# Loading the weights between later chunks of x, one shifted group sum, and score vectors formed by quarters inside the pass

## The reference

```python
# x: [1, R=128, C=192, E=192] fp32; 12 heads of D=16; weights E x E
xn = group_norm(x)                          # 32 groups of 6 channels; mean and variance over R, C and the group
q0 = xn[:, 0] @ Wq_s ; Ks = xn @ Wk_s       # tied row attention: one query row per column i
sw = softmax over r of (q0[i,h] . Ks[r,i,h]) / sqrt(D)
Q  = (xn @ Wq) * scaling * sw ; K = xn @ Wk ; V = xn @ Wv
attn = softmax over j of sum_r,d Q[r,i,h,d] K[r,j,h,d]   # 192 x 192 for each head
out = x + sum_j attn[h,i,j] V[r,j,h,d]
```

## Time and profile before

| | |
|---|---|
| median of 3 runs | 636.46 us (630.15 to 636.69) |
| profiled execution | 634.45 us, of which the span from the first to the last instruction is 632.7 us |
| busy: PE, DVE, ACT, POOL | 83%, 62%, 46%, 39% |
| statistics (to the last `bn_stats`) | 0 to 79.6 us |
| group sums, scale and shift | 79.6 to 91.9 us |
| row queries and score vectors | 91.9 to 127.6 us |
| pass of 24 chunks | 127.6 to 342.1 us |
| logits, attention, the second half | 342.1 to 632.7 us |

### The profile page before, as it was taken

The page is one execution under the profiler, slowest core; times in us unless marked ns, Lnnn a source line. Parts: engine busy times, 40 slices in busy tenths (PEclk is TensorE's granted clock), DMA queues, the critical chain, the costliest instruction groups (busy, mean ns, idle before and its releaser), DMA issues.

```text
span 632.7 us, 13676 instructions
## 1 busy us (share of the span) xinstructions
PE 526.1 (83%) x5131; PEld 398.9 (63%) x5131; DVE 394.9 (62%) x969; ACT 290.9 (46%) x658; POOL 244.8 (39%) x282
## 2 busy tenths in 40 slices
PE   1688568988888888888888999949599997999994
PEld 0678454634444444444446998838499997998773
DVE  0469935366677667776665566928257673667963
ACT  0279622456767676766753122323246562223242
POOL 2002004236665665566532000628245563000684
PEclk9879955589999999999998999969789998999987
DMA  6879401215665556547876999999877756899998
GB/s 172 322 259 366 174 1 50 94 58 156 195 200 168 162 172 200 185 163 154 200 150 108 291 289 270 300 341 271 272 247 257 251 199 150 267 294 289 301 271 228
DMA packets 183607, 134.40 MB, mean 212 GB/s; under 512 B 168256, under 2 KB 170240, under 8 KB 183552
## 3 DMA queue, kind: packets, MB, share of 16 engines
q1 hardware_dynamic: 131200, 113.26, 58.9%
q10 hardware_dynamic: 52352, 20.40, 12.9%
HBM read 77.02 MB, written 56.62 MB: 211 GB/s over the span
## 4 chain that ended last, share of the span: by engine, by line
PE 56%; DVE 24%; ACT 5%; issue 5%; ACTq 4%; POOL 3%; DMA 2%; DVEq 0%; POOLq 0%; SPq 0%
PE PS L1009 16%; PE PS L1017 8%; PE PS L1100 6%; DVE EXTRA L662 5%; DVE BIG L724 5%; DVE EXTRA L778 4%; PE PS L1130 3%; PE PS L1134 3%; PE PS L1133 3%; PE PS L1132 3%; PE PS L1131 3%; DVE BIG L888 3%; PE PS L970 2%; DVE BIG L781 2%; PE PS L910 2%
## 5 line engine op out<-in xcount | busy, mean ns | idle before, releaser
L1009 PE MATMUL PS<-WP,EXTRA 128*128 128x384 f16 (+1 forms) x1152 | 162.2, 290 | 7.3 <-DMA EXTRA<-xt_scratch 7.3
L1009 PEld LDWEIGHTS PS<-WP,EXTRA 128*128 128x128 f16 x1152 | 100.3, 100 | 50.8 <-issue 17.8
L416 POOL TENSOR_TENSOR EXTRA<-BIG,EXTRA 128x512 f16<-128x512 f32 x72 | 83.6, 1164 | 89.1 <-ACT EXTRA L505 89.1
L1100 PE MATMUL PS<-BIG,EXTRA 128*128 128x256 f16 x768 | 88.9, 278 | 11.5 <-ACT EXTRA L642 11.2
L450 POOL TENSOR_TENSOR BIG<-BIG,EXTRA 64x512 f32<-64x512 f32 x36 | 45.1, 1265 | 136.4 <-DVE BIG L888 111.4
L1100 PEld LDWEIGHTS PS<-BIG,EXTRA 128*128 128x128 f16 x768 | 75.8, 100 | 23.7 <-issue 12.8
L1017 PE MATMUL PS<-WP,EXTRA 64*128 64x384 f16 (+1 forms) x1152 | 82.6, 287 | 0.0
L422 POOL TENSOR_TENSOR BIG<-EXTRA,BIG 128x192 f16<-128x192 f32 x96 | 53.1, 553 | 66.8 <-ACT BIG L558 66.8
L775 DVE TENSOR_TENSOR EXTRA<-PS,SW 128x192 f32<-128x192 f32 x96 | 34.1, 355 | 61.2 <-ACT BIG L552 61.0
L1017 PEld LDWEIGHTS PS<-WP,EXTRA 64*128 64x128 f16 x1152 | 48.1, 95 | 30.4 <-issue 18.0
L549 ACT CAST EXTRA<-PS 128x384 f16<-128x384 f32 x96 | 45.8, 477 | 44.4 <-PE PS L1017 35.2
(11 more groups left out here) (162 smaller groups left out, 945.1 us busy)
## 6 DMA issues: line engine op xcount, KB each, us to landing
EXTRA<-in_x SPq DMA_DIRECT2D x28, 768.0 KB, 6.6
xt_scratch<-EXTRA SPq DMA_DIRECT2D x24, 768.0 KB, 3.4
EXTRA<-xt_scratch SPq DMA_DIRECT2D x24, 768.0 KB, 4.3
v_scratch<-EXTRA SPq DMA_DIRECT2D x32, 384.0 KB, 5.1
BIG<-v_scratch SPq DMA_DIRECT2D x16, 768.0 KB, 6.6
BIG<-in_x SPq DMA_DIRECT2D x12, 768.0 KB, 9.3
out_x<-BIG ACTq DMA_DIRECT2D x12, 768.0 KB, 6.7
v_scratch<-EXTRA SPq DMA_DIRECT2D x32, 192.0 KB, 4.3
```

Source lines behind the costliest of these rows:

```text
L416: pool.tensor_tensor(tt[:, t, 1, :].rearrange("p (q n) -> p q n", n=P), raw(c, t), tt[:, t, 0, :].rearrange("p (q n) -> p q n", n=P), ALU. ...
L1009: ins = mm(outs[a], xt[:, t, s, q * P:(q + 1) * P], WP[:, t, w, wc], start=first and j == 0, stop=last and j == 2, skip_group_check=True)
L1100: ins = mm(po[:, :, a, :], stationary, moving, start=j == 0, stop=j == len(terms) - 1)
```

## The change

- SP issues six chunks of x, then Wq_s, Wk_s, row 0 of x and the sequence mask, then the other chunks; the residue masks come after all chunks. ACT issues Wq and Wk first, Wv after the copy of chunk 1. Second copies of part of Wq_s and Wk_s are dropped.
- Work on the weights moves to chunks 7 to 20 of the statistics; PE forms the group matrices after chunks 2 to 4. PE waits for the maxima after chunk 9, for their diagonal after 11, for ACT's scaling after 16 and, in a new wait, for DVE's read of the transposed Wk_s after 18.
- The mean of chunk 0 by group serves as a shift. Sums and sums of squares of the shifted means go through one group sum (`s12`, two columns), and the variance subtracts the square of the mean.
- PE has 16 and 8 matmuls of 512 columns without use of their result ahead of the group sum and behind it (`keep_awake`).
- Only the first quarter of the score vectors is made before the pass. Quarters 1 to 3 follow the last piece of chunks 1, 3 and 5, with `queries_by_head` and `u_low` on DVE, `u_high` on ACT, and two turns each in the rotation of the three pairs of banks (`TAKERS`). The row queries are kept in SBUF (`QROW`).
- `low0` is split into `weighted_q` and `kv_low0`, so that chunk 0 can form low parts before its weights are there. The three tiles of `normalise_x`, now four chunks ahead, stand behind pieces 1, 2 and 3. `xn_high` opens the chunk on ACT. The transposed scores, maximum and exponent of chunk c+1 are made in chunk c (before: in chunk c-1, but for the exponent). POOL's order changes.

```diff
             for c in range(NCH):
-                if c == 1:
-                    sp.wait_ge(s_wld, 16 * N_WEIGHTS)
                 when(sp, s_tr, c - NSLOT + 1)
                 sp.dma_start(XR[c % NSLOT], xs[:, c * CI:(c + 1) * CI, :].rearrange("r c e -> r (c e)")
                              ).then_inc(s_x[c % NSLOT], 16)
+                if c == NSLOT - 1:
+                    sp.wait_ge(s_zero, 4)
+                    for k, w in enumerate((wqs, wks)):
+                        sp.dma_start(WS[:, k, 0, :], w[0:P, :]).then_inc(s_wld, 16)
+                        sp.dma_start(WS[0:E1, k, 1, :], w[P:E, :]).then_inc(s_wld, 16)
+                    sp.dma_start(X0[:, 0, :], xs[0, 0:P, :]).then_inc(s_params, 16)
+                    sp.dma_start(X0[0:E1, 1, :], xs[0, P:C, :]).then_inc(s_params, 16)
+                    sp.dma_start(seq_i[:, :], seq_mask.rearrange("a r -> r a")).then_inc(s_params, 16)
+            sp.dma_start(res_i[:, 0:1], res_mask[:, 0:P].rearrange("a r -> r a")).then_inc(s_res, 16)
+            sp.dma_start(res_i[0:E1, 1:2], res_mask[:, P:C].rearrange("a r -> r a")).then_inc(s_res, 16)
+            sp.dma_start(row_i, res_mask.partition_broadcast(P).rearrange("p a r -> p (a r)")).then_inc(s_res, 16)
...
-            for c in range(3):
-                for t in range(3):
-                    xn_low(c, t)
+            xn_low(0, 0)
+            xn_low(0, 1)
+            xn_low(1, 0)
+            xn_low(1, 1)
+            for t in range(3):
+                xn_low(2, t)
             for c in range(NCH):
-                for g in range(NQ):
-                    if c or g:
-                        q_low0(c - (g == 0), (g - 1) % NQ)
-                    if g < 3 and c + 3 < NCH:
-                        xn_low(c + 3, g)
+                if c + 3 < NCH:
+                    xn_low(c + 3, 0)
+                if c:
+                    q_low0(c - 1, NQ - 1)
+                if c + 3 < NCH:
+                    xn_low(c + 3, 1)
+                q_low0(c, 0)
+                if c + 3 < NCH:
+                    xn_low(c + 3, 2)
+                q_low0(c, 1)
+                q_low0(c, 2)
             q_low0(NCH - 1, NQ - 1)
...
                 copy_raw(c)
-                if c == 4:
+                if c == 1:
...
+                if 2 <= c < 5:
+                    act.wait_ge(s_gp, c - 1)
+                    nc.scalar.copy(GM[:, c - 2, :, :], PS[:, 7, 0:3 * P].rearrange("p (b n) -> p b n", b=3)
+                                   ).then_inc(s_gm, 1)
+                if 12 <= c < 15:
                     act.wait_ge(s_rv, 1)
-                    for k in range(3):
-                        nc.scalar.mul(W[:, k, :, :], W[:, k, :, :], rv5[:, k:k + 1])
...
+                if c == 15:
                     for k in range(2):
-                        ins = nc.scalar.mul(WS[:, k, :, :], WS[:, k, :, :], rv5[:, 3 + k:4 + k])
...
-                if c == 7:
-                    act.wait_ge(s_wsc, 1)
-                    for col0, w, w0, n in W_PARTS:
-                        ins = nc.scalar.copy(WP[:, :, 0, col0:col0 + n], W[:, w, :, w0:w0 + n])
-                    ins.then_inc(s_wh, 1)
+                        nc.scalar.mul(WS[:, k, :, :], WS[:, k, :, :], rv5[:, 3 + k:4 + k]).then_inc(s_wsc, 1)
+                if 16 <= c < 21:
+                    act.wait_ge(s_wsc, 5)
+                    col0, w, w0, n = W_PARTS[c - 16]
...
             scores_low(1)
-            row_weights(0)
-            for c in range(NCH):
+            q_high0(0, 1)
+            q_high0(0, 2)
+            kv_high0(0, 3)
+            exponent(1)
+            scores_low(2)
...
-                    if c or g:
-                        q_high0(c - (g == 0), (g - 1) % NQ)
-                    if g == 0 and c + 3 < NCH:
-                        xn_high(c + 3)
-                    if g == 1 and c + 1 < NCH:
-                        row_weights(c + 1)
-                    if g == 2 and c + 2 < NCH:
-                        scores_low(c + 2)
+                kv_high0(c, 1)
+                q_high0(c, 0)
+                if c + 2 < NCH:
+                    scores_low(c + 2)
+                kv_high0(c, 2)
+                q_high0(c, 1)
+                if c + 1 < NCH:
+                    row_weights(c + 1)
+                kv_high0(c, 3)
+                if ("u", (c + 1) // 2, 0) in TAKERS and c % 2:
+                    u_high((c + 1) // 2)
+                q_high0(c, 2)
...
+            for c in range(NCH):
                 ins = statistics(c)
-                if c == 8:
+                if c == 0:
+                    step(ins)
+                    v.tensor_tensor(s0, sv[:, :, 0, 1], sv[:, :, 1, 1], ALU.add).then_inc(s_s0, 1)
+                if c == 7:
+                    dve.wait_ge(s_mm0, 1)
+                    v.tensor_scalar(shift, GS[:, :, 0], 1.0 / first, None, ALU.mult)
+                    dve.wait_ge(s_wld, 16 * N_WEIGHTS)
+                    dve.wait_ge(s_zero, 4)
+                    v.tensor_reduce(mx5[:, 0:3], W.rearrange("p w t n -> p w (t n)"), AX.X, ALU.max,
+                                    apply_absolute_value=True)
+                    v.tensor_reduce(mx5[:, 3:5], WS.rearrange("p w t n -> p w (t n)"), AX.X, ALU.max,
+                                    apply_absolute_value=True).then_inc(s_wmax, 1)
+                if c == 9:
+                    dve.wait_ge(s_wmaxT, 1)
...
+                    v.tensor_reduce(head8, ident[:, :].rearrange("p (h s) -> p h s", s=D), AX.X, ALU.add)
+                if c == 14:
...
+                    step(v.tensor_scalar(seqscale, seqscale, seq01, 1.0 / D ** 0.5 / U_SCALE, ALU.mult, ALU.mult))
+                if c == 17:
                     dve.wait_ge(s_wkt, 1)
                     v.tensor_scalar(WKT[:, 0, :], PS[:, 7, 0:256], U_SCALE, None, ALU.mult)
                     v.tensor_scalar(WKT[0:E1, 1, :], PS[0:E1, 7, 256:512], U_SCALE, None,
                                     ALU.mult).then_inc(s_wkr, 1)
             step(ins)
...
-            v.tensor_scalar(var, GS[:, 1, :], 1.0 / (n_sub * members), EPS, ALU.mult, ALU.add).then_inc(s_var, 1)
+            step(v.tensor_tensor(DM, sv[:, :, :, 1], shift.unsqueeze(2).to_broadcast([P, 3, K]), ALU.subtract))
+            v.tensor_reduce(s12[:, :, 0], DM, AX.X, ALU.add)
+            step(v.tensor_tensor(DM2, DM, DM, ALU.mult))
+            v.tensor_reduce(s3, sv[:, :, :, 2], AX.X, ALU.add)
+            step(v.tensor_reduce(s2, DM2, AX.X, ALU.add))
+            v.scalar_tensor_tensor(s12[:, :, 1], s2, float(n_sub), s3, ALU.mult, ALU.add).then_inc(s_st, 1)
+            dve.wait_ge(s_mm, 1)
+            step(v.tensor_scalar(mean, GS[:, :, 0], 1.0 / members, None, ALU.mult))
+            v.tensor_scalar(var, GS[:, :, 1], 1.0 / (n_sub * members), EPS, ALU.mult, ALU.add)
+            step(v.tensor_tensor(s2, mean, mean, ALU.mult))
+            v.tensor_tensor(var, var, s2, ALU.subtract).then_inc(s_var, 1)
+            v.tensor_tensor(mean, mean, shift, ALU.add)
             dve.wait_ge(s_std, 1)
...
-            queries_by_head()
-            normalise_x(1)
+            normalise_x(1, range(2))
+            queries_by_head(0)
+            first_low(0)
+            normalise_x(1, (2,))
+            keep_queries()
             u_low(0)
...
-            for c in range(NCH):
-                if c + 3 < NCH:
-                    normalise_x(c + 3)
-                for g in range(NQ):
-                    low0(c, g)
-                    if g == 0 and c + 1 < NCH:
-                        normalise_weights(c + 1)
-                    if g == 2 and c + 2 < NCH:
-                        score(c + 2)
+            normalise_x(4)
+            normalise_weights(1)
+            score(2)
+            for c in range(1, NCH):
+                if c + 1 < NCH:
+                    score_max(c + 1)
+                weighted_q(c, 0)
+                kv_low0(c, 0)
+                if c + 1 < NCH:
+                    normalise_weights(c + 1)
+                weighted_q(c, 1)
+                kv_low0(c, 1)
+                if c + 4 < NCH:
+                    normalise_x(c + 4, (0,))
+                k = (c + 1) // 2
+                vectors = c % 2 and k < UG
+                if vectors:
+                    queries_by_head(k)
+                weighted_q(c, 2)
+                kv_low0(c, 2)
+                if c + 4 < NCH:
+                    normalise_x(c + 4, (1,))
                 if c + 2 < NCH:
-                    score_max(c + 2)
+                    score(c + 2)
+                weighted_q(c, 3)
+                kv_low0(c, 3)
+                if vectors:
+                    u_low(k)
+                if c + 4 < NCH:
+                    normalise_x(c + 4, (2,))
...
+                for b in range(3):
+                    for t in range(3):
+                        ins = mm(GS[:, b, 0:n], GM[:, t, b, :], s[:, t:t + 1] if n == 1 else s[:, t, :],
+                                 start=t == 0, stop=t == 2)
+                return ins
+
+            def keep_awake(n):
+
```

(79 more changed lines are left out.)

267 lines of the change are left out of this document (148 added, 119 removed).

## The result

| | before | after |
|---|---|---|
| median of the runs | 635.8 us | 625.4 us |
| range of the runs | 630.2 to 636.7 | 623.7 to 628.1 |
| profiled execution, time and span | 634.45, 632.7 | 624.96, 623.2 |
| granted TensorE clock, mean | 0.919 | 0.941 |

The ratio is 0.989, with an interval of 0.984 to 0.993. The forecast was 612: a gain of 22 to 24 us, of which 10 came.

A forecast was written before the change was run, and what follows sets the result against it. Bounds: a late DVE start in the statistics, then PE's small fp32 products, then a loop of waits in the pass with no engine full. 634.45 - 15.9 - 21.2 + 14.2 = 611.6, predicted 612 us; range 588 to 628.

The forecast's parts named there:

- the statistics: First stage: DVE starts at about 9.9 us instead of 24.65 and ends at 68, bounds 60 and 82.
- the group sum: Last statistics to row queries: 8 us instead of 12.3; row queries start at 76, 15.9 earlier.
- Start of the pass: Row queries to first piece of chunk 1: 25.8 us instead of 47.0, 21.2 saved.
- The pass from chunk 1, +14.2: Chunks 1 to 6 cost 10.7 us more, chunks 7 to 20 cost 6.0, the last two gain 2.5.
- The period: Steady chunk of the pass: loop through xn_high 8.33 plus DVE waits for POOL of 0.75 and 0.28, 9.35 us.
- The pair of chunks with a quarter: Chunks 1 to 6: two chunks with a quarter of the score vectors take 22.3 us instead of 18.7.
- No lock, or line 764 alone free, 599: Rival for the pass: DVE and POOL miss each other, 589, or line 764 doesn't wait, 599; chance 0.26.
- Nothing much, 634: Rival for the pass: the DVE-POOL lock costs 1 us more per chunk, 10.3 in 22 chunks; chance 0.07.
- The front doesn't shrink as it should, 626: Rival for the statistics: PE at the low clock throughout, stage ends at 82 instead of 68; chance 0.1.
- The likeliest case, 603 to 620: The prediction's own case for the whole kernel, 612 us; chance 0.5.
- rival of 7 in 100: Pass: four DVE instructions each wait out a POOL instruction, period 12.3 us, kernel 672; chance 0.07.
- What would show it: Trace signs over statistics, sum and pass, among them period 9.3 and pairs of 22 us; wrong if the chain runs through PE.

The follow-up runs named there:

- e3: Changed kernel's front (loads, maxima, group sum, idle matmuls) with the start and pass of the kernel before; 618.9 us, 0.976 of the kernel before.
- e5: Changed kernel with ACT's exponent written to PSUM and read from there by the division of the row weights; 610.8 us.
- e8: Changed kernel without the 16 and 8 idle matmuls around the group sum; 630.9 us.
- e2: Changed kernel with ACT's cast of x (xn_high) one place later, behind the casts of the chunk's first group; 604.4 us.
- e9: Changed kernel with all four quarters of the score vectors made ahead of the pass; 636.4 us.
- e4: Changed kernel with all three normalise_x behind the chunk's first group and xn_high behind the casts of the second; 592.9 us.
- e7: Changed kernel with all three normalise_x behind the chunk's first group, the cast of x left in front; 632.4 us.
- e6: e4 with SP storing a chunk's values before the transposed x of three chunks ahead; 581.2 us.

## Why the prediction was wrong

**What bounds the kernel, the statistics, the group sum.** Right. DVE started at 10.0 (9.9), the statistics ended at 69.8 (68), DVE idled 9.9 us in them (the bound was 12). The stop at chunk 18 was 2.8 us of PE (3 to 4 forecast) with 3.9 of idle DVE behind it; of the others, where the forecast had 2, the one at 9 was 2.4, at 11 PE didn't wait, and the old one for ACT's scaling, now at 16, was 1.4. The sum took its 4.01 at the low clock, and 8.5 us lie between statistics and row queries (8). Row queries came 13.6 earlier in the trace (15.9), and e3's trace has the same 13.6 at the first logits.

**Start of the pass.** Near, but too long in its parts: 23.3 from row queries to chunk 1 against 25.8, which made good the 2.3 lost ahead of it. The terms that the prediction lists add up to 26.1 to 29.3, not to its "24 to 27". Queries and spreading took 3.0 (4.8), the quarter 3.7 (3.3 to 6.5), the rest 16.5 (18). That the quarter ran at the high clock was luck: in the profiles of e5 to e8 it didn't, and in e8 it took 6.50.

**The pass from chunk 1, +14.2: this term failed.** It was +26.5. With -13.6 for the front, -23.7 for the start and +1.3 for the rest, the span fell by 9.5 instead of 22.9. The mechanism of the period is the one forecast, in both parts: the loop through `xn_high` (e2) and whole-instruction turns of DVE and POOL at line 764, now 854 (e5). The term was sized too small, in four places:
- The addition itself. Three pairs of 22.3 are 66.9, which is 13.4 over 6 x 8.92; the prediction has 10.7, near 3 x (22.3 - 18.7), and 18.7 is two chunks at the new period, not at the old one. Added up rightly its own terms give +16.9 and 614: 2.7 of the 12 us missed are this slip.
- The period, 9.65 in place of 9.35: 3.9 in 13 chunks, and 1.0 more in the three at a mean clock of 0.83. The wait at the weights measured 0.82 (0.75), that of the first `normalise_x` 0.54 (0.28). "The other two find gaps" was right. The two prices weren't independent, as I had summed them: with the first gone (e5) the `normalise_x` are 0.17 a chunk shorter too, and the lists are right to 0.05.
- The pair of chunks with a quarter, 23.85 in place of 22.3. Of the 1.55, 0.6 is the longer period, twice; the other 0.95 is the quarter, which adds 4.55 to a chunk (14.20 - 9.65) where the forecast has 3.6 (22.3 - 18.7). In chunk 3 the clock was 0.50 from 133 to 136 us, and PE's part of the quarter took 4.2 there, against 3.7 at the high clock in chunk 1 and 3.4 forecast.
- Chunk 1, 16.2 between casts, 2 more than the other chunks with a quarter. The chain shows `queries_by_head` at 1.31 at 110.42, where the two later instances take 0.70, and projections at a granted clock of 0.76 from 100 to 107. Neither was in the sum. The second is the one that tells: from the cast to the second copy of the chunk (line 599) it is 4.94 us (101.78 to 106.72), in chunk 3 2.57 (127.62 to 130.19). In e9, which spreads no queries in the pass, chunk 1 still takes 12.29 where a chunk takes 9.66, with PE at 0.50 from 126 to 131. Whether it is the low clock alone, or also that no projection had run ahead, isn't separated.

The four places make 14.3; from chunk 20 on the pass took 2.1 less than the forecast, which leaves the 12.

**Rivals.** "No lock, or line 764 alone free, 599" had its test in e5: with the line free the kernel takes 610.8, so the figure was 12 too low: the slip, the last two places, and in its profile the first quarter at the low clock. "Nothing much, 634: the lock costs 1 more per chunk" was the nearest in kind: it cost 0.3 more. "The front doesn't shrink as it should, 626" came nearest in number, by accident: its statistics were to end at 82 and ended at 69.8. The likeliest case, 603 to 620, missed; the range held only because the rivals widened it. I gave the time of the likeliest case to a loop whose closing waits were each read from one row; a bound of a whole `xn_low` on each in turn would have given 9.35 + 0.35 + 0.8 = 10.5 as the far end of the period, not a separate rival of 7 in 100.

**What would show it.** Last `bn_stats`, one group of 18 at the sum (the 4.01 above), chunk 1 near 102, chain through `xn_high` and the long median of line 854: as said. Period 9.3 and pairs of 22: not. A chain through PE, named as a sign of being wrong, appears in chunks of 7 to 20 at the low clock alone.

## What to carry to other kernels

When DVE and POOL both work from SBUF, place DVE's instructions against POOL's start times, not against DVE's own gaps: the same three `normalise_x`, in the same place of DVE's list, cost 1.6 us a chunk where POOL starts behind them (e4) and 3.4 where it starts beside them (e7). If one can't be moved, let its input come from PSUM. And after moving one instruction, look at the in-order queues behind its consumers: the store of v (e6) was two engines away from the cast.

## What the runs showed of the hardware

- A DVE instruction of 0.28 us costs 1.10 when it starts 0.13 behind a POOL instruction of 1.15, and a two-input instruction from SBUF does the same (1.17 beside 0.35). From PSUM all 24 stay at 0.35.
- PE busy 26.58 of 26.60 us on small fp32 products ran at the 1.2 GHz level throughout (e9, and e3 the same at 84.7 to 111.3). A quarter of them between f16 projections ran at 1.00 in chunk 1 of the changed kernel (112 to 116 us) and at 0.50 in one chunk of e5 (163 to 166 us), with PE busy throughout in both.
- Chunks of the same work, in one execution, took 9.65 us at a mean granted clock of 1.00 and 9.87 to 10.14 at 0.83, where the chain went over to PE.
